# Layer 1 of a two-layer recurrent kernel: fp32 products of whole operands in place of three-term split products

## What is computed

```python
left  = gelu(xn @ Wl + bl)
r_in  = xn @ Wr + br
u     = causal_conv4(r_in, conv_w) + conv_b          # per channel, 320 channels
r, i  = sigmoid(u @ Wa + ba), sigmoid(u @ Wi + bi)   # the gate products
log_a = -8.0 * softplus(-lam) * r
a     = exp(log_a)
drive = sqrt(max(1 - exp(2 * log_a), 1e-12)) * (i * u)
h[t]  = a[t] * h[t-1] + drive[t]                     # scan over 512 tokens
s     = (left * h) @ Wo + bo                         # the output product
g     = silu(_L1_ffn_ref(xn, ...))                   # the edit branch: a choice of 1 of 8
out   = x + s * g
```

## Time and profile before

| | before |
|---|---|
| median of 3 runs | 458.74 us (455.46 to 459.42) |
| span of the profiled execution | 457.3 us |
| PE (matmul) busy | 351.9 us, 77%, 2088 instructions |
| PE weight loads busy | 254.3 us, 56% |
| DVE busy | 313.0 us, 68%, 857 instructions |
| ACT busy | 180.0 us, 39%, 319 instructions |
| POOL busy | 196.9 us, 43%, 133 instructions |
| DMA | 30.20 MB, mean 66 GB/s |

### The profile page before, as it was taken

The page is one execution under the profiler, slowest core; times in us unless marked ns, Lnnn a source line. Parts: engine busy times, 40 slices in busy tenths (PEclk is TensorE's granted clock), DMA queues, the critical chain, the costliest instruction groups (busy, mean ns, idle before and its releaser), DMA issues. The chain is left out here.

```text
span 457.3 us, 6207 instructions
## 1 busy us (share of the span) xinstructions
PE 351.9 (77%) x2088; PEld 254.3 (56%) x2088; DVE 313.0 (68%) x857; ACT 180.0 (39%) x319; POOL 196.9 (43%) x133
## 2 busy tenths in 40 slices
PE   0795785838508989999999999999656686994852
PEld 0584574725306656675666665666545574772742
DVE  4867699639408885888346664674769959859893
ACT  1312623602011422234445344544203675865720
POOL 5562652913213652536255536564354342304026
PEclk9998888859955998999999999999895979795895
DMA  8000299979890412212101141110015000000002
GB/s 272 28 26 7 95 136 181 135 204 124 171 107 23 114 37 44 71 34 75 39 36 36 58 140 36 36 34 1 2 54 189 1 1 0 0 1 1 0 0 92
DMA packets 23066, 30.20 MB, mean 66 GB/s; under 512 B 3171, under 2 KB 18187, under 8 KB 23035
## 3 DMA queue, kind: packets, MB, share of 16 engines
q1 hardware_dynamic: 19003, 18.80, 21.9%
q10 hardware_dynamic: 4032, 11.01, 7.8%
HBM read 24.99 MB, written 4.82 MB: 65 GB/s over the span
## 5 line engine op out<-in xcount | busy, mean ns | idle before, releaser
L380 POOL TENSOR_TENSOR wl<-wr,wh 128x768 fp32r<-128x768 f32 x28 | 51.3, 1833 | 76.7 <-ACT wh L466 60.4
L522 ACT ACTIVATE PT<-bank 128x512 f32<-128x512 f32 (+1 forms) x88 | 44.3, 557 | 39.5 <-PE bank L946 39.4
L679 DVE TENSOR_REDUCE mx<-bank 128x1 f32<-128x384 f32 (+3 forms) x88 | 52.3, 635 | 10.7 <-PE bank L927 10.4
L925 PE MATMUL bank<-KS,QS 112*128 112x128 bf16 (+3 forms) x128 | 34.5, 323 | 30.4 <-DVE mx L679 21.8
L149 PE MATMUL bank<-xh,wh 128*128 128x512 f32 x112 | 51.5, 460 | 4.0 <-DVE gb L804 1.4
L418 POOL TENSOR_TENSOR gl<-gb,gh 128x512 fp32r<-128x512 f32 x28 | 36.2, 1293 | 37.4 <-DVE gh L811 24.9
L790 DVE SCALAR_TENSOR_TENSOR s<-th,bank 128x512 f32<-128x512 f32 x28 | 19.2, 685 | 41.0 <-ACT th L529 41.0
L150 PE MATMUL bank<-xl,wh 128*128 128x512 f32 x112 | 46.3, 413 | 0.0
L151 PE MATMUL bank<-xh,wl 128*128 128x512 f32 x112 | 46.2, 413 | 0.0
L925 PEld LDWEIGHTS bank<-KS,QS 112*128 112x128 bf16 x128 | 13.0, 103 | 46.8 <-DVE mx L679 32.1
L149 PE MATMUL bank<-wh,gh 128*128 128x256 f32 x112 | 37.6, 335 | 0.5 <-POOL gl L418 0.5
(11 more groups left out here) (249 smaller groups left out, 924.0 us busy)
## 6 DMA issues: line engine op xcount, KB each, us to landing
wr<-in_w_chunks_dram ACTq DMA_DIRECT2D x28, 384.0 KB, 3.2
QS<-parts_dram SPq DMA_DIRECT2D x12, 256.0 KB
KS<-parts_dram SPq DMA_DIRECT2D x12, 256.0 KB, 9.3
parts_dram<-wp SPq DMA_DIRECT2D x4, 384.0 KB, 3.5
parts_dram<-x SPq DMA_DIRECT2D x4, 384.0 KB, 15.3
acts<-in_w_ai_dram SPq DMA_DIRECT2D x1, 1152.0 KB, 6.4
x<-in_x_dram SPq DMA_DIRECT2D x2, 512.0 KB, 6.4
KS<-in_x_dram SPq DMA_DIRECT2D x1, 1024.0 KB, 5.6
```

The lines of the kernel that those rows point to most:

```text
L380: pool.tensor_tensor(wl[:, s % 3, :, :], wr[:, s % 2, :, :], wh[:, s % 3, :, :].bitcast(F32), ALU.subtract).then_inc(wl_ready, 1)
L522: act.activation(PT[:, k % 8, 0:n], bank[k % 2][:, 0:n], ACT.Exp, scale=float(DH) ** -0.5).then_inc(P_ready, 1)
L679: dve.tensor_reduce(mx[:, b * TB + i, heads[0]:heads[-1] + 1], bank[k % 2][:, 0:len(heads) * n].rearrange("p (h n) -> p h n", n=n), AX.X, ...
L925: pe.matmul(out, QS[0:R_MAX, h, b * S + i * P:b * S + (i + 1) * P], KS[0:R_MAX, h, b * S:b * S + n], start=True, stop=False)
```

## The change

The gate products and the output product of layer 1 are taken as one fp32 matmul each of the whole `w_ai` and `u`, and of `prod` and `w_o`. The casts and subtractions of these four operands are gone, with their tiles and semaphores. The split of `w_lr` and `xn` for the two branches stays, as does everything in layer 0. `w_ai` and `w_o` have tiles of their own, so `decays` waits for no split; the product of the recurrence goes to a new tile `prod`, and in batch 1 DVE waits for `O_ready` (the first output product has been issued and done) before it writes it.

```diff
@@ POOL
-            for k, (lo, raw, hi) in enumerate(((w_lr_l, w_lr, w_lr_h), (w_ai_l, w_ai, w_ai_h), (w_o_l, w_o, w_o_h))):
-                pool.wait_ge(wh_ready, k + 1)
-                pool.tensor_tensor(lo[:, :, :], raw, hi[:, :, :].bitcast(F32), ALU.subtract).then_inc(wl_ready, 1)
...
-            rests_of_u(0)
-            rests_of_u(1)
-            rests_of_products(0)
-            rests_of_products(1)
+            pool.wait_ge(wh_ready, 1)
+            pool.tensor_tensor(w_lr_l[:, :, :], w_lr, w_lr_h[:, :, :].bitcast(F32), ALU.subtract).then_inc(wl_ready, 1)
@@ ACT
-                act.wait_ge(wl_ready, 3)
...
-            act.wait_ge(w_in["ai"], 16)
-            act.copy(w_ai_h[:, :, :], w_ai).then_inc(wh_ready, 1)
-            split_u(0)
...
-            act.wait_ge(w_in["o"], 16)
-            act.copy(w_o_h[:, :, :], w_o).then_inc(wh_ready, 1)
...
-            split_u(1)
...
-            split_products(0)
...
-            split_products(1)
@@ DVE, recurrence(b)
-                    if b:
-                        dve.wait_ge(pl_ready, p + 1)
...
-                    dve.tensor_tensor(drv[:, p, :], ti[:, p, :], left[:, b, p, :], ALU.mult).then_inc(prod_ready, 1)
+                    if b:
+                        dve.wait_ge(O_ready, 1)
+                    dve.tensor_tensor(prod[:, p, :], ti[:, p, :], left[:, b, p, :], ALU.mult).then_inc(prod_ready, 1)
@@ PE, gates(b, which)
-                pe.wait_ge(wl_ready, 2)
+                pe.wait_ge(w_in["ai"], 16)
...
-                            pe.wait_ge(ul_ready, b * HT + k + 1)
-                            ins = split_matmul(pe, bank[3 * g + p][:, :], w_ai_h[:, k, w], w_ai_l[:, k, w],
-                                               uh[:, b, k, :], ul[:, b, k, :], k == 0, k == HT - 1)
+                            pe.wait_ge(u_ready, b * HT + k + 1)
+                            ins = pe.matmul(bank[3 * g + p][:, :], w_ai[:, k, w], u[:, b, k, :],
+                                            start=(k == 0), stop=(k == HT - 1))
@@ PE, mix_out(b)
-                    pe.wait_ge(pl_ready, b * HT + k + 1)
+                    pe.wait_ge(prod_ready, b * HT + k + 1)
                     for i in range(TB):
-                        ins = split_matmul(pe, bank[6 + i // 2][:, i % 2 * D:(i % 2 + 1) * D],
-                                           ph[:, k, tokens(i)], pl[:, k, tokens(i)], w_o_h[:, k, :], w_o_l[:, k, :],
-                                           k == 0 and i % 2 == 0, k == HT - 1, skip=True)
+                        ins = pe.matmul(bank[6 + i // 2][:, i % 2 * D:(i % 2 + 1) * D], prod[:, k, tokens(i)],
+                                        w_o[:, k, :], start=(k == 0 and i % 2 == 0), stop=(k == HT - 1),
+                                        skip_group_check=True)
```

More of the change, by code:

```diff
@@ L1092, in layer1 @@
         w_lr_l = m.sb("w_lr_l", [P, KD, 2 * HP], F32R)
[L1093 to L1096, removed]
+        w_ai = m.sb("w_ai", [P, HT, 2 * HP])
+        w_o = m.sb("w_o", [P, HT, D])
         w_f = m.sb("w_f", [P, KD, FW])
@@ L1119, in layer1 @@
         u = m.sb("u", [P, B, HT, S])
-        uh = m.sb("uh", [P, B, HT, S], F32R)
-        ul = m.sb("ul", [P, B, HT, S], F32R)
         left = m.sb("left", [P, B, HT, S])
@@ L1125, in layer1 @@
         drv = m.sb("drv", [P, HT, S])
-        ph = m.sb("ph", [P, HT, S], F32R)
-        pl = m.sb("pl", [P, HT, S], F32R)
+        prod = m.sb("prod", [P, HT, S])
         w_lr = drv[:, :, :].rearrange("p k n -> p (k n)").rearrange("p (k n) -> p k n", n=2 * HP)
-        w_ai = acts[:, 0:2, :].rearrange("p a n -> p (a n)")[:, 0:HT * 2 * HP].rearrange("p (k n) -> p k n", n=2 * HP)
-        w_o = acts[:, 2, 0:HT * D].rearrange("p (k n) -> p k n", n=D)
         Y = m.sb("Y", [P, T, FW])
@@ L1158, in layer1 @@
         wh_ready, wl_ready = sem("wh"), sem("wl")
-        R_ready, rin_ready, u_ready, uh_ready, ul_ready = (
-            sem(n) for n in ("R", "rin", "u", "uh", "ul"))
+        R_ready, rin_ready, u_ready = (sem(n) for n in ("R", "rin", "u"))
         vec_ready, vec_exp, vec_dve, vec_ln, half_done = (sem(n) for n in ("vecr", "vexp", "vdve", "vln", "half"))
@@ L1163, in layer1 @@
             sem(n) for n in ("A", "I", "ta", "ti", "dec", "sqd", "om", "beta"))
-        L_ready, left_ready, prod_ready, ph_ready, pl_ready, O_ready = (
-            sem(n) for n in ("L", "left", "prod", "ph", "pl", "O"))
+        L_ready, left_ready, prod_ready, O_ready = (sem(n) for n in ("L", "left", "prod", "O"))
         F_ready, F_read, fc_ready, fcm_ready, fb_ready, fb_read = (
@@ L1189, in _ @@
             load(vec[:, :, :], a["vecs"], "vec")
-            load(w_ai, a["w_ai"].rearrange("(k p) n -> p k n", p=P), "ai")
-            load(w_o, a["w_o1"].rearrange("(k p) n -> p k n", p=P), "o")
+            load(w_ai[:, :, :], a["w_ai"].rearrange("(k p) n -> p k n", p=P), "ai")
+            load(w_o[:, :, :], a["w_o1"].rearrange("(k p) n -> p k n", p=P), "o")
             load(w_g[:, :], a["w_g"], "selc")
@@ L1211, in _ @@
                 pool.tensor_tensor(rstd[:, tb], ve[:, tb], mhalf[:, tb], ALU.pow).then_inc(rstd_ready, 1)
-            for k, (lo, raw, hi) in enumerate(((w_lr_l, w_lr, w_lr_h), (w_ai_l, w_ai, w_ai_h), (w_o_l, w_o, w_o_h))):
-                pool.wait_ge(wh_ready, k + 1)
-                pool.tensor_tensor(lo[:, :, :], raw, hi[:, :, :].bitcast(F32), ALU.subtract).then_inc(wl_ready, 1)
[L1215 to L1224, removed]
-                    if b:
-                        pool.wait_ge(O_ready, 1)
-                    pool.tensor_tensor(pl[:, p, :], drv[:, p, :], ph[:, p, :].bitcast(F32),
-                                       ALU.subtract).then_inc(pl_ready, 1)
-            rests_of_u(0)
-            rests_of_u(1)
-            rests_of_products(0)
-            rests_of_products(1)
+            pool.wait_ge(wh_ready, 1)
+            pool.tensor_tensor(w_lr_l[:, :, :], w_lr, w_lr_h[:, :, :].bitcast(F32), ALU.subtract).then_inc(wl_ready, 1)
             for t in range(T):
@@ L1260, in convolution_in @@
                                    bias=vec[:, 2, p:p + 1]).then_inc(tap_ready, 1)
[L1262 to L1265, removed]
             def left_gelu(b):
@@ L1298, in roots_and_inputs @@
                                    bias=vec2[:, 5, p:p + 1]).then_inc(ti_ready, 1)
[L1300 to L1305, removed]
             def transposed_selection():
```

2 lines of the change are left out of this document (1 added, 1 removed).

## The result

The changed kernel ran in 443.4 us (median of 4 runs, 441.63 to 444.86) beside 457.1 us for the kernel before (4 runs, 454.16 to 459.42): a ratio of 0.973, with a 95% interval of 0.967 to 0.980. The difference is 13.7 us; forecast were 13.5, or 445.2 us from the median of three runs known then, with a range of 441 to 452. In all that follows a median is over all runs, while a ratio leaves out slow ones, those over 1.5% above the fastest of their kernel.

What follows compares the result with a forecast made beforehand. The prediction took layer 1's DVE work, stretched by waiting for POOL, to bound the kernel. Its terms down the chain summed to -13.5 us, from 458.74 to 445.2 us, with a range of 441 to 452.

Steps and rivals of the forecast that it cites:

- Step 2: Edit products on PE follow with hardly a pause, 4.5 us for 6.25; with two small products ahead, -1.9 us.
- rival B: PE's clock stays low longer, in gates, mix and tail: 452 us, from 449 to 453; chance 0.17.
- Step 4: DVE's constants L1378, L1381, L1382 fall from about 1.2 to 0.17-0.2 us, -2.9; slower A tiles add 0.4.
- Step 7: 27 gate products make PE late for the edit's first input, at 405.2 us; PE gives back 1.0 us.
- Step 5: One fp32 gate product on PE takes 0.86 us at the high clock, +0.16 a product.
- Step 9: First mix takes 6.9 us for 5.6, with four of 12 products at the low clock: +1.3 us.
- Step 10: First `I` tile of batch 1 needs 3 gate products, 2.6 us for 2.1: +0.5.
- Step 11: Second recurrence loses two stretched scans, -2.0 us; POOL's first four output additions run earlier beside DVE, +1.5.
- Step 12: Tail loses ACT's cast, POOL's subtraction and hops, -2.0 us; last four products take 3.0 us, no change.
- C: DVE's long instructions are not POOL's doing and stay: within 1%, near 459 us; chance 0.04.
- D: Slower: fp32 products never bring PE's clock up, time near 471 us; chance 0.02.
- E: More than forecast, under 441 us: no pause lowers the clock and POOL's additions are free; chance 0.05.

Runs made afterwards that it cites:

- experiment 1: Changed kernel with all removed ACT casts and POOL subtractions put back, results unused, in smaller tiles: 455.36 us, ratio 1.002 to the kernel before.
- experiment 5: Changed kernel with one useless POOL subtraction of 128x2304, begun after the third `cv`: 446.03 us, one execution.
- experiment 6: Changed kernel with three POOL memsets of 128x2304, begun after the third `cv`: 443.76 us, one execution.
- experiment 8: Changed kernel run once more unaltered, 6 runs: 443.3 us, ratio 0.971 to the kernel before.
- experiment 10: Changed kernel with useless PE matmuls, five ahead of the edit products and eight ahead of the first mix: 441.89 us, ratio 0.973.
- experiment 9: Changed kernel with the edit's transposes and first two pairs of products ahead of batch 1's decay gates on PE: 445.18 us, ratio 0.979.
- experiment 7: Changed kernel with POOL's four output additions of batch 0 kept behind the second recurrence: 442.36 us, ratio 0.976.
- experiment 3: Changed kernel with the mix split again, so only the gates are unsplit: 447.19 us, ratio 0.981 to the kernel before.
- experiment 11: Changed kernel with the edits of experiments 7, 9 and 10 together: 439.67 us, ratio 0.961 to the kernel before.
- experiment 12: Experiment 11's kernel with eight more useless PE matmuls ahead of the gates: 439.81 us, ratio 0.958 to the kernel before.
- mix-only kernel: Changed kernel with the gates split again, so only the output product is unsplit: 453.83 us, ratio 0.989 to the kernel before.
- experiment 2: Changed kernel with ACT's casts alone put back, results unused, no subtraction on POOL: 444.08 us, ratio 0.977 to the kernel before.

## Why the prediction was right, and where it was not

- **Step 1** (L1403, -4.83): -4.8 where the third `u` ends. Experiments 1, 5 and 6 show the cause.
- **Step 2** (edit products, -1.9): mis-sized, it brought -0.7. The step took 4.5 us for "hardly a pause"; 1.25 us of pause were left, since L1528 waits for `fcm`, which DVE makes behind the third `u`, and the clock fell all the same: 5.84 us. Experiments 8 and 10 show the 4.5 (4.56 and 4.57) when it doesn't fall. The fault was to read a shorter pause as one that doesn't lower the clock, while rival B said for the gates that nothing in the trace tells how short is short enough.
- **Step 3** (L1419, L1420, -2.0): -2.2; they are at 0.69, and a small neighbour, L1374, is down to 0.23 too.
- **Step 4** (constants, with ACT waiting for PE by 0.4): -2.5, which is what the two terms, -2.9 and +0.4, make. The sum went on with -11.3 for -11.2, a slip of 0.1 that step 7 ends, since it is reckoned from absolute times. The three constants shrank by 3.15 us (3.65 to 0.50) and not by 2.9; ACT stood 0.34 us for the third A tile.
- **Step 5** (0.86 us a product): measured 0.86. The Trainium skill (FP8 and Floating Point Precision, TensorE Precision Notes) gives four passes to true fp32; taken as four for three of the fp32r matmuls, a product would have been 0.93. The ratio to three fp32r matmuls (0.70) is 1.23 here, not 1.33, so the row it was read from was the better guide.
- **Step 6** (-2.0): -2.0, every scan at 1.22.
- **Step 7** (PE late by 1.0): +1.0; DVE stands 0.95 us for L1551, and experiment 9 takes it away.
- **Step 8** (-0.6): -0.6.
- **Step 9** (mix 6.9 us, +1.3): 6.89, and +1.1 at its end; the low clock lasted 3.0 us of it, where four products at that level, 3.4 us, were taken.
- **Step 10** (first `I` tile, +0.5): it doesn't show in the changed kernel, because the additions cover it. Experiment 7 shows it: DVE idle for 0.67 us for ACT, where it was 0.19 before.
- **Step 11** (two scans -2.0, additions +1.5): from the fourth scan's start to the sixth's end 7.8 us for 9.9, -2.1; the additions stretch DVE by 2.0 us, 1.2 of which count by experiment 7. With step 10: -0.3, where 0.0 was forecast.
- **Step 12** (the tail, -2.0): mis-sized as well, -2.9. From the end of the last recurrence product to the start of `left` it was 5.0 us (445.23 to 450.23) and is 2.08 (431.45 to 433.53). The step took the last mix at 3.0 us, between its two levels; it ran at the full clock, in 2.03 (431.50 to 433.53).

The mechanism and the path were right: DVE's stretched instructions are the larger part of the gain and the tail's two hops the smaller. Two terms were mis-sized. Step 2 gave 1.2 us too much, step 12 some 0.9 too little and steps 10 and 11 another 0.3. The two large ones are the same question, whether PE's clock falls at a pause, and the forecast missed in both places; that they cancel is luck. So is the agreement to 0.2 us in the medians: their ratio's interval, 0.967 to 0.980, leaves about 3 us to either side, and in layer 1 alone the gain was 14.0.

The rivals: **C** fell with experiments 1, 5 and 6. **B** came in part: of ten executions with unsplit gates and the same pause ahead of them, four ran low at their start (experiments 3, 7, 8, 11), for 3.4 us each time and not 5.6. It costs 1.7 us in the gates (25.11 for 23.41). Between the two executions of the changed kernel layer 1 differs by 1.0: the second lost 1.7 at the gates and 0.6 more at the first mix (7.33 us for 6.72), and had not lost the 1.3 of the edit products. **D** did not come: 54 fp32 records in a row ran at the full clock. **E** needed what experiment 12 had to build.

## What to carry to other kernels

Look for one line of DVE with two durations, and lay POOL's timeline beside it: a POOL subtraction of two tiles in SBUF cost DVE up to its own length where it met DVE work on SBUF (4.8 us beside 5.04, 3.8 beside 4.34, 3.1 beside 3.53), also when nobody waited for its result. So work "moved to the idle engine" may be worth less than leaving it out, and when it runs counts: the same three `ul` cost 2.0 us before and nothing in the mix-only kernel, where they ran earlier. A product of unsplit fp32 operands was only 1.2 times as dear on PE (0.86 for 0.70 us) as three products of parts, and worth it here, where PE had slack and the making of the parts held up DVE. Shorten PE's pauses, but do not count on the full clock behind them: here it held from the branch products to the last mix only in the kernel that filled three of them.

## What the runs showed of the hardware

- **Writing alone does not block.** Three memsets of 128x2304 (6.18 us) left DVE's 1.53 us as they were; one subtraction of that size (4.34 us) made 5.30 of them. Even instructions on 128x3 elements were blocked, 1.24 us for 0.16, and one of 128x256 with one tile and scalars as input, 3.51 for 0.41 beside `w_lr_l`. Three that read PSUM were not (0.28, 0.30 and 0.30 us beside the mix-only kernel's `ul`).
- **The length of a pause alone does not tell whether the clock falls.** Ahead of the edit products 1.18, 1.20, 1.24, 1.25 and 1.47 us lowered it (experiments 6, 2, 9, the changed kernel, experiment 3), 0.48 and 0.49 did not (experiments 8, 7). Ahead of the gates the same 1.92 to 1.94 us lowered it in four executions (experiments 3, 7, 8, 11) and not in six others; the changed kernel itself is on both sides. Its layer 1 took 101.4 and 102.4 us, and the clock makes the difference. In experiment 10 the clock fell 0.2 us after PE had gone back to unbroken work.
- **fp32 products** run at 0.43 us for 256 columns and 0.86 for 512 at the full clock, in two records each, while fp32r matmuls of 512 columns start 0.233 us apart.
- **The common part varies by more than the later edits gain:** layer 0, the same code, ended anywhere from 335 to 342 us, which is why places were measured from layer 1's start.
